# The experts' second layer with the tokens stationary, and the last 32 rows of each expert as quarter rows

## The reference

```
cap = int(1.25 * T / E)                  # 4096 tokens, 32 experts: 160 rows an expert
idx = argsort(-score, axis=0)[:cap].T    # the 160 tokens of each expert
xe  = xf[idx]                            # (32, 160, 512)
up  = einsum('eci,eji->ecj', xe, w_up)   # 2 x 1024 hidden units
gate, upv = split(up, 2)
hact = silu(gate) * upv
ye  = einsum('ecj,eoj->eco', hact, w_down)
out = zeros.at[idx].add(w * ye)
```

## Time and profile before

| | us |
|---|---|
| median of the runs | 1921.09 |
| the profiled execution | 1920.14 |
| its span | 1918.3 |
| TensorE busy | 1596.3 (83%) |
| L836 (first layer), TensorE busy | 637.8 |
| L849 (second layer), TensorE busy | 321.5 |

### The profile page before, as it was taken

The page is one execution under the profiler, slowest core; times in us unless marked ns, Lnnn a source line. Parts: engine busy times, 40 slices in busy tenths (PEclk is TensorE's granted clock), DMA queues, the critical chain, the costliest instruction groups (busy, mean ns, idle before and its releaser), DMA issues.

```text
span 1918.3 us, 28344 instructions
## 1 busy us (share of the span) xinstructions
PE 1596.3 (83%) x10882; PEld 1370.2 (71%) x10882; DVE 796.2 (42%) x1757; ACT 496.7 (26%) x1197; POOL 282.3 (15%) x371
## 2 busy tenths in 40 slices
PE   3478898898887542379999999999999999999970
PEld 1245555555555422279999999999999999999970
DVE  4648889889887646821111111111111111111117
ACT  1544654754745310011111111111111111111100
POOL 2001011111111110001111111111111111111112
PEclk9697898998997765689999999999999999999995
DMA  5023032132310152016666666666666666666519
GB/s 143 8 59 100 12 109 66 45 110 67 88 45 30 37 227 91 0 70 254 232 254 230 254 230 254 229 255 230 254 229 255 229 255 228 256 228 256 176 15 350
DMA packets 88670, 309.71 MB, mean 161 GB/s; under 512 B 42326, under 2 KB 42332, under 8 KB 79260
## 3 DMA queue, kind: packets, MB, share of 16 engines
q1 hardware_dynamic: 78876, 287.87, 40.0%
q0 software_dynamic: 9728, 20.98, 6.2%
HBM read 272.52 MB, written 36.31 MB: 161 GB/s over the span
## 4 chain that ended last, share of the span: by engine, by line
PE 73%; DVE 14%; ACT 7%; issue 4%; DMA 1%; POOL 1%; SPq 0%; POOLq 0%; DVEq 0%; ACTq 0%
PE bank L836 33%; PE bank L849 17%; PE bank L557 6%; PE bank L693 3%; DVE arena L1164 2%; DVE arena L1492 2%; PE banks L647 2%; PE banks L815 2%; PE banks L631 1%; PE bank L559 1%; ACT arena L994 1%; PE banks L816 1%; DVE arena L1621 1%; DVE arena L1158 1%; ACT arena L905 1%
## 5 line engine op out<-in xcount | busy, mean ns | idle before, releaser
L836 PE MATMUL bank<-arena 128*128 128x160 f32 x4608 | 637.8, 299 | 0.6 <-issue 0.6
L836 PEld LDWEIGHTS bank<-arena 128*128 128x128 f32 x4608 | 630.0, 190 | 1.1 <-issue 0.7
L1604 DVE TENSOR_TENSOR arena<-arena,bank 128x160 f32<-128x160 f32 x256 | 82.1, 321 | 828.0 <-ACT arena L1117 828.0
L849 PE MATMUL bank<-arena 128*128 128x160 f32 x2304 | 321.5, 300 | 1.0 <-DVE arena L1606 1.0
L849 PEld LDWEIGHTS bank<-arena 128*128 128x128 f32 x2304 | 313.8, 190 | 2.4 <-issue 1.2
L1117 ACT ACTIVATE arena<-bank 128x160 f32<-128x160 f32 x288 | 87.4, 303 | 562.4 <-PE bank L836 562.4
L1775 POOL DMA_INDIRECT acc_rows<-arena,keep x64 | 95.2, 1488 | 831.4 <-DVE arena L1593 795.1
L557 PE MATMUL bank<-arena 128*128 128x512 f32 x256 | 135.3, 678 | 58.8 <-DVE arena L1164 58.8
L557 PEld LDWEIGHTS bank<-arena 128*128 128x128 f32 x256 | 53.9, 218 | 123.6 <-issue 88.3
L1123 ACT ACTIVATE arena<-bank 128x320 f32<-128x320 f32 x64 | 28.0, 437 | 292.4 <-PE bank L849 292.4
L1164 DVE SCALAR_TENSOR_TENSOR arena<-arena 128x512 f32<-128x512 f32 x128 | 95.8, 748 | 3.4
(11 more groups left out here) (225 smaller groups left out, 1764.2 us busy)
## 6 DMA issues: line engine op xcount, KB each, us to landing
arena<-in_wup SPq DMA_DIRECT2D x32, 4096.0 KB, 12.5
arena<-in_wdn SPq DMA_DIRECT2D x32, 2048.0 KB, 8.5
arena<-in_aup SPq DMA_DIRECT2D x32, 512.0 KB, 11.6
arena<-in_xT SPq DMA_DIRECT2D x8, 1024.0 KB, 5.4
arena<-in_kT SPq DMA_DIRECT2D x8, 1024.0 KB, 7.4
arena<-in_v SPq DMA_DIRECT2D x32, 256.0 KB, 7.7
x_rows<-arena SPq DMA_DIRECT2D x8, 1024.0 KB, 4.4
acc_rows<-arena SPq DMA_DIRECT2D x8, 1024.0 KB, 6.9
```

Of the source, the lines that this page charges most:

```text
L836: m = pe.matmul(u[:, g * CAP:(g + 1) * CAP], w, xeT[:, c, :], start=(c == 0), stop=(c == C - 1))
L849: m = pe.matmul(Db[k][:, c * CAP:(c + 1) * CAP], w, hact[:, j, :], start=(j == 0), stop=(j == J))
L1604: dve.tensor_tensor(hact[:, j, :], sg[k], u, ALU.mult).then_inc(up_v(f"mul{j}"), 1)
```

## The change

`down` now holds the tokens stationary. For each of the 9 chunks, one product has `hact`'s 128 tokens stationary and the whole 512-wide row block of `w_down` moving, into `Yb[0]` as token rows. Behind it the last 32 tokens are stationary four times, once for each group of 32 columns of the array, and each group has another 128-feature quarter of the same weights moving; the four results lie on partitions 0 to 31, 32 to 63, 64 to 95 and 96 to 127 of `Yb[1]`. So the last 32 rows appear as 128 quarter rows of 128 features. `rows_out` of TensorE, `yT`, the `Db` banks and ScalarE's copies of them go. `rows_in` takes five 128x128 transposes for the former four and four, and the second DMA of gather and scatter moves 128 quarter rows of 512 bytes instead of 32 rows of 2 KB. To have row numbers and weights on all 128 partitions, eight small products spread the second column of the two tables over the four column groups, and VectorE adds the number of the quarter.

```diff
+            pe.wait_ge(*lf_v.at("rows", b0))
+            for k, src in enumerate((tid_l, w_l)):
+                rest = src.rearrange("p (e k) -> p e k", k=2)[0:CAP2, :, 1]
+                for c in range(C):
+                    m = pe.matmul(Bb[CAP2 * c:CAP2 * (c + 1), k * NE:(k + 1) * NE], ident[0:CAP2, 0:CAP2], rest,
+                                  start=True, stop=True)
+            m.then_inc(lf_t("spread"), 1)
...
-                    for c in range(2):
-                        ch = slice((2 * k + c) * P, (2 * k + c + 1) * P)
-                        pe.transpose(Xb[k][:, c * CAP:c * CAP + P], xg[e.slot][:, 0, ch], ident)
-                        m = pe.transpose(Xb[k][:, c * CAP + P:(c + 1) * CAP], xg[e.slot][0:CAP2, 1, ch],
-                                         ident[0:CAP2, 0:CAP2])
+                    for c in range(C * k, C + k):
+                        at = c % C * P
+                        m = pe.transpose(Xb[k][:, at:at + P], xg[e.slot][:, c * P:(c + 1) * P], ident)
                     m.then_inc(xr_t(f"x{k}"), 1)
...
                 pe.wait_ge(ld_wd[e.slot], e.landed())
                 pe.wait_ge(ld_ad[e.slot], e.landed())
                 pe.wait_ge(*up_v.at(f"mul{J}", e))
-                for k in range(2):
-                    pe.wait_ge(*dn_a.at(f"d{k}", e - 1))
-                    for c in range(2):
-                        ch = slice((2 * k + c) * P, (2 * k + c + 1) * P)
-                        for j in range(J + 1):
-                            w = wd[e.slot][:, j, ch] if j < J else ad[e.slot][:, ch]
-                            m = pe.matmul(Db[k][:, c * CAP:(c + 1) * CAP], w, hact[:, j, :], start=(j == 0), stop=(j == J))
-                    m.then_inc(dn_t(f"d{k}"), 1)
-            def rows_out(e):
...
+                pe.wait_ge(*yr_v.at("y1", e - 1))
+                for j in range(J + 1):
+                    w = wd[e.slot][:, j, :] if j < J else ad[e.slot]
+                    m = pe.matmul(Yb[0][:, :], hact[:, j, 0:P], w, start=(j == 0), stop=(j == J))
+                    if j == J:
+                        m.then_inc(yr_t("y0"), 1)
                     for c in range(C):
+                        r = pe.matmul(Yb[1][CAP2 * c:CAP2 * (c + 1), 0:P], hact[:, j, P:CAP],
+                                      w[:, c * P:(c + 1) * P], start=(j == 0), stop=(j == J))
+                r.then_inc(yr_t("y1"), 1)
...
+            for c in range(C):
+                dve.memset(quarter[CAP2 * c:CAP2 * (c + 1)], float(c))
...
-            dve.scalar_tensor_tensor(idx_l, tid_l, -1.0, emp, ALU.add, ALU.add).then_inc(lf_v("idx"), 1)
+            dve.scalar_tensor_tensor(tid_l, tid_l, -1.0, emp, ALU.add, ALU.add).then_inc(lf_v("rows"), 1)
+            dve.wait_ge(*lf_v.at("rows", b0))
+            dve.tensor_copy(idx_l, tid_l)
+            dve.wait_ge(*lf_t.at("spread", b0))
+            dve.tensor_copy(w_l.rearrange("p (e k) -> p e k", k=2)[:, :, 1], Bb[:, NE:2 * NE]).then_inc(lf_v("spread_w"), 1)
+            dve.wait_ge(*lf_v.at("spread_w", b0))
+            dve.tensor_scalar(idx_l.rearrange("p (e k) -> p e k", k=2)[:, :, 1], Bb[:, 0:NE], float(C), quarter,
+                              ALU.mult, ALU.add).then_inc(lf_v("idx"), 1)
...
-                dve.tensor_scalar(yy[e.slot][0:CAP2, 1, :], Yb[1][0:CAP2, :], w[0:CAP2, 1:2], None, ALU.mult)\
+                dve.tensor_scalar(yy[e.slot][:, D:], Yb[1][:, 0:P], w[:, 1:2], None, ALU.mult).then_inc(yr_v("y1"), 1)
...
-                for k, n in enumerate((P, CAP2)):
-                    pool.indirect_dma_start(out=acc_d,
+                for k, (cols, rows) in enumerate(((slice(0, D), acc_d), (slice(D, D + P), acc_q))):
+                    pool.indirect_dma_start(out=rows,
```

More of the change, by code:

```diff
@@ L146, in decoder_kernel @@
     acc_d = nc.dram_tensor("acc_rows", (NTOK + CAP, D), F32, kind="Internal").ap()
+    x2_q, acc_q = (t.rearrange("n (g d) -> (n g) d", g=C) for t in (x2_d, acc_d))
     ctx = ExitStack()
@@ L186, in decoder_kernel @@
         w_l = keep.take(2 * NE)
+        quarter = keep.take(1)
         idx_l = keep.take(2 * NE, dt=I32)
@@ L373, in decoder_kernel @@
         room3 = Room(arena, ROOM, late)
-        xg = [room3.take(2, D) for _ in range(2)]
+        xg = [room3.take(D + P) for _ in range(2)]
         xeT = room3.take(C, CAP)
@@ L377, in decoder_kernel @@
         hact = room3.take(J + 1, CAP)
-        yT = room3.take(C, CAP)
-        yy = [room3.take(2, D) for _ in range(2)]
+        yy = [room3.take(D + P) for _ in range(2)]
         room4 = Room(arena, ROOM)
@@ L386, in decoder_kernel @@
         Ub = bank[0:2]
-        Db = bank[2:4]
         Xb = bank[4:6]
@@ L408, in decoder_kernel @@
         li_t = steps("list_tensor", [f"m{i}" for i in range(2 * NT // LG)], 0)
-        lf_v = steps("listfin_vector", ["tid", "w", "empty", "fill", "idx"], 0)
+        lf_v = steps("listfin_vector", ["tid", "w", "empty", "fill", "rows", "spread_w", "idx"], 0)
+        lf_t = steps("listfin_tensor", ["spread"], 0)
         up_t = steps("up_tensor", [f"up{j}" for j in range(J + 1)], 2)
@@ L414, in decoder_kernel @@
         xr_a = steps("rowsin_scalar", ["x0", "x1"], 2)
-        dn_t = steps("down_tensor", ["d0", "d1"], 2)
-        dn_a = steps("down_scalar", ["d0", "d1"], 2)
         yr_t = steps("rowsout_tensor", ["y0", "y1"], 2)
@@ L491, in load_expert @@
                 sp.dma_start(au[s], aup_d[pair]).then_inc(ld_au[s], 16)
-                sp.wait_ge(*dn_t.at("d1", e - 2))
+                sp.wait_ge(*yr_t.at("y1", e - 2))
                 sp.dma_start(wd[s], wdn_d[e.line(1)]).then_inc(ld_wd[s], 16)
@@ L842, in down @@
                 pe.wait_ge(*up_v.at(f"mul{J}", e))
-                for k in range(2):
-                    pe.wait_ge(*dn_a.at(f"d{k}", e - 1))
-                    for c in range(2):
-                        ch = slice((2 * k + c) * P, (2 * k + c + 1) * P)
-                        for j in range(J + 1):
-                            w = wd[e.slot][:, j, ch] if j < J else ad[e.slot][:, ch]
-                            m = pe.matmul(Db[k][:, c * CAP:(c + 1) * CAP], w, hact[:, j, :], start=(j == 0), stop=(j == J))
-                    m.then_inc(dn_t(f"d{k}"), 1)
-            def rows_out(e):
-                pe.wait_ge(*dn_a.at("d1", e))
-                for k in range(2):
-                    pe.wait_ge(*yr_v.at(f"y{k}", e - 1))
-                    for c in range(C):
[L857 to L861, removed]
+                pe.wait_ge(*yr_v.at("y1", e - 1))
[4 more added lines that the diff above has]
+                        m.then_inc(yr_t("y0"), 1)
+                    for c in range(C):
+                        r = pe.matmul(Yb[1][CAP2 * c:CAP2 * (c + 1), 0:P], hact[:, j, P:CAP],
+                                      w[:, c * P:(c + 1) * P], start=(j == 0), stop=(j == J))
+                r.then_inc(yr_t("y1"), 1)
             def expert(e, first, last_):
[L864 to L867, removed]
+                for j in range(J + 1):
                     up(e, j)
@@ L874, in _ @@
             run_experts(pe, expert)
-            rows_out(Batch(0, NE - 1))
         @block.scalar
@@ L1102, in rows_in @@
                 act.wait_ge(*up_t.at(f"up{J}", e - 1))
[L1103 to L1107, removed]
+                act.wait_ge(*xr_t.at("x0", e))
+                act.activation(xeT[:, :, 0:P], Xb[0][:, :].rearrange("p (c t) -> p c t", c=C), ACT.Copy)\
+                    .then_inc(xr_a("x0"), 1)
+                act.wait_ge(*xr_t.at("x1", e))
+                act.activation(xeT[:, :, P:CAP], Xb[1][:, 0:P].rearrange("p (c t) -> p c t", c=C), ACT.Copy)\
+                    .then_inc(xr_a("x1"), 1)
             def expert(e, first, last):
@@ L1119, in expert @@
                     rows_in(e + 1)
[L1120 to L1125, removed]
             rows_in(b0)
@@ L1590, in rows_out @@
                 dve.wait_ge(*yr_t.at("y0", e))
-                dve.tensor_scalar(yy[e.slot][:, 0, :], Yb[0][:, :], w[:, 0:1], None, ALU.mult).then_inc(yr_v("y0"), 1)
+                dve.tensor_scalar(yy[e.slot][:, 0:D], Yb[0][:, :], w[:, 0:1], None, ALU.mult).then_inc(yr_v("y0"), 1)
                 dve.wait_ge(*yr_t.at("y1", e))
-                dve.tensor_scalar(yy[e.slot][0:CAP2, 1, :], Yb[1][0:CAP2, :], w[0:CAP2, 1:2], None, ALU.mult)\
-                    .then_inc(yr_v("y1"), 1)
+                dve.tensor_scalar(yy[e.slot][:, D:], Yb[1][:, 0:P], w[:, 1:2], None, ALU.mult).then_inc(yr_v("y1"), 1)
             def expert(e, first, last):
@@ L1598, in expert @@
                     if j == 0:
-                        dve.wait_ge(*dn_t.at("d1", e - 1))
+                        dve.wait_ge(*yr_t.at("y1", e - 1))
                     k = (e.slot * (J + 1) + j) % 2
@@ L1761, in gather @@
                 hold(pool)
-                for k, n in enumerate((P, CAP2)):
-                    pool.indirect_dma_start(out=xg[e.slot][0:n, k, :], out_offset=None, in_=x2_d,
```

(12 more changed lines are left out.)

## The result

The changed kernel takes 1963.27 us (median of 4 runs, 1961.74 to 1963.87) against 1920.85 us for the kernel before in the same set: ratio 1.0219, 95% interval 1.0202 to 1.0237, slower. The forecast was 1965. The profiled execution's span grew from 1918.3 to 1961.6 us, by 43.3; the sum of the prediction was 43.7.

The account below looks back on a forecast made before the run. TensorE's stream was taken as the bound. Second layer +90.9, rows in and wait -18.3, rows out -27.3, ends +1.6 - 1.2 - 2.0 give +43.7 us: 1965 us, own range 1953 to 1976, 8 in 10 1945 to 1985.

Parts of the forecast that it names:

- The price of the change of tiling: In `down`, going from full array into column groups and back costs 0.335 us a chunk, range 0 to 0.42.
- The first rival: In `down`, changing tiling costs little behind a full product, as L860 behind L858; kernel 1868 us; chance 0.06.
- The second rival: In `down`, drains exist but the full product's weight load hides in them: -30 us, 1935 us; chance 0.07.
- the third: In `down`, second half pass exposed or exit longer, 0.04 to 0.085 us a chunk: 1977 to 1989 us; chance 0.12.
- The fourth: In `down`, short groups run one after another, +0.63 us a chunk, +181 us: 2146 us; chance 0.03.
- The wait for `mul8`: Before `down`, shorter `rows_in` uncovers this wait: start 1.15 us after the last `up8` product's start, gaining 0.67 an expert.
- The fifth rival: Before `down`, the wait for `mul8` costs nothing, -0.47 x 31: 1950 us; chance 0.04.
- The ends: Ahead of and behind the experts: +1.6 us spreading tables, -1.2 first `rows_in`, -2.0 after the last `down`.
- the forecast's +1.6: Ahead of the experts: small products 0.85, two VectorE operations 0.45, memsets about 0.3 us; between 0.8 and 3.
- The first `rows_in`: At half clock, five transposes take 2.0 us where it took 3.23 with its copies: -1.2 us.
- The scatter and gather changes: On GpSimd and DMA, 128 descriptors for 32 cost nothing under GpSimd's 25 us waiting; without it up to 2 us an expert.

Follow-up runs that it names:

- two reorderings: Changed kernel with an expert's column groups behind all nine large products, 1878.3 us; and with them behind every third large product, 1899.51 us.
- The row part alone: Changed kernel's quarter rows and five transposes with the earlier kernel's second layer, last 32 rows through an identity product into four column groups: 1902.5 us.
- the one-change kernel: Changed kernel with an expert's nine large products first and all nine sets of column groups behind them: 1878.3 us.
- the single group: Changed kernel with only the first of the four column groups computed: 1955.21 us.
- the kernel with both edits: Changed kernel with all large products before all groups, and the wait for `mul8` moved to just before the last chunk's large product: 1859.85 us.

## Why the prediction was right

**The price of the change of tiling** was the step that decided, and it held, as a mechanism and piece by piece: 0.335 a chunk predicted, 0.332 from the times of two reorderings and 0.335 from their traces; 1.413 us a chunk, 1.41 measured; 12.72 us for the second layer, 12.71 measured. The reading that made it possible was start to start in the attention stage, not busy time.

**The first rival** rested on L860. The row part alone shows why it misled: what follows the full array at no cost is the transpose; a plain product in the groups is charged at the same place. The second rival (weight load hidden) falls with the 697 ns of L851, the third (second half pass or exit dearer) with the one-change kernel and the chunk's own starts: half passes stand 0.109 us apart, and from the last half pass to the large product it is 0.202 us, 0.109 and 0.093. The fourth (one group after another) falls with the single group.

**The wait for `mul8`** was predicted at 1.15 us after the last first-layer product and came at 1.10 on average. The fifth rival falls. The mechanism is the predicted one, but the closeness is in part luck: 1.15 was picked between two rows. The upper one, the last expert's 1.25, was taken for the bare wait without `rows_in`, while the changed kernel has 1.25 also in experts that do have `rows_in` and stand outside the loop. Had I priced `rows_in` by its streaming alone (-1.14 an expert instead of -0.67, and no exposed load), the forecast would have been 17 us lower.

**The ends.** The timeline ahead of the experts and behind them in the changed kernel answers to the earlier trace rows:

```profile
827.99 0.23 DVE L1572 SCALAR_TENSOR_TENSOR keep<-keep,arena 128x64 f32<-128x64 f32 x1
828.25 0.20 DVE L1574 CAST keep<-keep 128x64 int32<-128x64 f32 x1
...
828.27 0.33 PE L810 MATMUL bank<-keep 32*32 32x32 f32 x16 [1.07 <-DVE keep L1572]
828.68 0.19 DVE L1576 COPY keep<-bank 128x32 f32<-128x32 f32 x1 [0.23 <-PE bank L810]
828.91 0.25 DVE L1578 TENSOR_SCALAR keep<-bank,keep 128x32 int32<-128x32 f32 x1
...
834.78 1.33 PE L822 MATMUL banks<-keep,arena 128*128 128x128 f32 x5 [6.17 <-DMA arena<-x_rows,keep]
...
836.86 4.38 PE L841 MATMUL bank<-arena 128*128 128x160 f32 x17 [0.75 <-issue]
...
1904.98 0.43 PE L855 MATMUL banks<-arena 128*32 128x128 f32 x8
1905.16 0.75 DVE L1587 TENSOR_SCALAR arena<-banks,keep 128x512 f32<-128x512 f32 x1 [12.76 <-PE banks L851]
1905.83 0.34 DVE L1589 TENSOR_SCALAR arena<-banks,keep 128x128 f32<-128x128 f32 x1
```

From L1572's end (828.22) to L1578's end (829.16) the spreading adds 0.94 us, where 1.3 were priced (16 records of 32x32 in 0.33 us and not 0.85). L1572 itself ends 0.66 us later than L1583 did, where 0.3 were priced for the memsets; those stand at 701.91, in 0.37 us. So the forecast's +1.6 (the first transposes came 1.69 later) is right by two errors that cancel, and by chance: among the traces of the variants, which share this part, the first product of the experts starts anywhere from 835.2 to 838.9 us. The first `rows_in` takes 2.08 us (2.0 predicted), and from the last record of the second layer (1905.41) to VectorE's end (1906.17) it is 0.76 (0.7 predicted). The scatter and gather changes cost nothing that shows inside the experts, as argued; behind the last VectorE operation the trace is 0.34 us longer. What they would cost without GpSimd's waiting, up to 2 us an expert in the prediction, no run shows.

In all, start to start between the two traces:

| | us |
|---|---|
| first product of the first expert (836.32 to 836.86) | +0.54 |
| 31 periods (992.63 to 1035.02) | +42.39 |
| last expert's first layer, which had held a `rows_out` | -0.77 |
| last expert's second layer, to its end (10.02 to 12.75) | +2.73 |
| from there to VectorE's end (2.69 to 0.76) | -1.93 |
| the rest | +0.34 |
| sum | +43.3 |

Of the 31 periods the first grew by 2.62 us and the others by 1.33 on average. In the first, 0.40 us came from the clock alone, which no term had: the first layer took 21.33 us from first to last start for 20.93, at a granted clock of 0.91 for 0.93 (later experts have 1.00). Against that stood the wait, taken 0.05 too long 31 times. No error was above 3 us.

## What to carry to other kernels

Products in column groups do run beside each other, but the way into them and back to full-array products has a fixed price, 0.33 us here for the pair, whether one, two, three or nine sets stand between (f32, 128 stationary columns outside, 32 inside): collect all work of one tiling behind all work of the other, and count the switches before the columns. A step that becomes shorter uncovers the wait that it hid; look for the bare wait at a place where the step is missing (here the last expert, which gave an upper bound: 1.25 us for 1.05 to 1.12 inside the loop), and move the wait to the first instruction that needs it.

## What was not expected of the hardware

The price splits as the rows of before said. It hardly depends on the number of groups in use (one group 1.39 us a chunk, four 1.41, the difference being the stagger), and not on how often it has been paid. Sixteen 32x32 records in the four column groups took 0.33 us from first start to last end; the estimate had been more than double. The gaps are invisible in busy time: PE shows 33.08 of 33.28 us busy with nine pairs of them in it. Nor does PEld's busy time tell: 24.23 us with nine changes, 25.35 of 30.13 us with one (the kernel with both edits). Only the starts do. And the time from `mul8`'s end to the second layer's start, 0.05, 0.13 or 0.25 us by the expert's place in the program, was not foreseen, and stays unexplained.
